# Softmax sums of a full attention: two running sums with every third tile added by an accumulating DMA, and three groups of totals on TensorE, in place of eight short sums and nine groups

## The reference

```python
qkv = (x @ qkv_w + qkv_b).reshape(Bw, Nw, 3, nh, dh)      # Nw = 3136 tokens, nh = 8 heads, dh = 32
q, k, v = (qkv[:, :, 0], qkv[:, :, 1], qkv[:, :, 2])
attn = jnp.einsum('bnhd,bmhd->bhnm', q * scale, k)
bias = jnp.transpose(rpb_table[rel_idx], (2, 0, 1))
attn = jax.nn.softmax(attn + bias[None], axis=-1)
out = jnp.einsum('bhnm,bmhd->bnhd', attn, v).reshape(Bw, Nw, Cd)
```

## Time and profile before

| | |
|---|---|
| median of 3 runs | 6850.28 us (6849.53 to 6852.86) |
| profiled execution, its own time | 6852.2 us |
| its span, first to last instruction | 6850.3 us |
| mean granted TensorE clock | 0.95 |
| PE busy | 5952.2 us (87%) |
| PE weight loads | 3529.1 us (52%) |
| DVE busy | 4462.8 us (65%) |
| ACT busy | 3207.0 us (47%) |
| POOL busy | 4402.5 us (64%) |

### The profile page before, as it was taken

How to read it: one execution, slowest core, us unless ns; L and a number is a source line. 1 busy time by engine, 2 the same in 40 slices (tenths; PEclk the granted TensorE clock), 3 DMA queues, 4 the chain that set the end, 5 groups by cost and what they waited for, 6 DMA issues and landing times. The chain is left out here.

```text
span 6850.3 us, 123297 instructions
## 1 busy us (share of the span) xinstructions
PE 5952.2 (87%) x37974; PEld 3529.1 (52%) x37974; DVE 4462.8 (65%) x8532; ACT 3207.0 (47%) x6574; POOL 4402.5 (64%) x1492
## 2 busy tenths in 40 slices
PE   2777767769999999999999999999999999442878
PEld 2666545545555555555555555555555554231555
DVE  2666633357777777777777777777777775684000
ACT  1444411106666665666666666666666666000111
POOL 0222222228888888888888888888888888443332
PEclk9999989969999999999999999999999999675988
DMA  1111144441101101111100100110110000332221
GB/s 38 45 42 44 39 140 163 155 124 44 32 15 33 46 15 33 30 32 33 30 24 24 46 24 23 33 39 23 33 32 20 17 15 8 104 112 65 46 47 24
DMA packets 217803, 323.95 MB, mean 47 GB/s; under 512 B 43392, under 2 KB 182628, under 8 KB 214244
## 3 DMA queue, kind: packets, MB, share of 16 engines
q1 hardware_dynamic: 201084, 295.76, 15.1%
q0 software_dynamic: 13568, 19.39, 1.5%
q10 hardware_dynamic: 2664, 2.62, 0.2%
HBM read 179.93 MB, written 137.35 MB: 46 GB/s over the span
## 5 line engine op out<-in xcount | busy, mean ns | idle before, releaser
L1193 DVE TENSOR_REDUCE tops<-ps_m 128x1 f32<-128x448 f32 (+1 forms) x5600 | 3120.5, 618 | 911.3 <-PE ps_m L1096 860.2
L1169 ACT ACTIVATE prob<-ps_s 128x448 f32<-128x448 f32 (+1 forms) x5600 | 2619.8, 550 | 1748.0 <-PE ps_s L1032 1708.7
L1002 POOL TENSOR_TENSOR tile_sum<-prob 128x1792 f32<-128x1792 f32 x448 | 1802.4, 4023 | 664.3 <-ACT prob L1169 664.0
L1032 PE MATMUL ps_s<-queries,keys 97*128 97x448 f32 (+1 forms) x5600 | 2200.2, 397 | 15.4 <-ACT prob L1169 7.6
L1096 PE MATMUL ps_m<-keys,queries 96*128 96x448 f32 (+1 forms) x5600 | 2092.2, 381 | 35.4 <-DMA keys<-k_parts 20.2
L1002 POOL TENSOR_TENSOR tile_sum<-tile_sum,prob 128x1792 f32<-128x1792 f32 x448 | 1807.8, 4035 | 31.8
L1032 PEld LDWEIGHTS ps_s<-queries,keys 97*128 97x128 f32 (+1 forms) x5600 | 1042.2, 187 | 1158.0 <-ACT prob L1169 660.7
L1048 PE MATMUL ps_o<-prob,values 128*32 128x448 f32 x11200 | 1343.1, 551 | 2.9 <-ACT prob L1169 1.2
L1096 PEld LDWEIGHTS ps_m<-keys,queries 96*128 96x128 f32 (+1 forms) x5600 | 1062.6, 190 | 240.2 <-DVE tops L1193 84.8
L257 POOL TENSOR_TENSOR logit<-logit,top 112x896 f32<-112x896 f32 x112 | 188.4, 1683 | 557.3 <-DVE top L374 557.3
L1060 PE MATMUL ps_d<-tile_sum,ones 128*32 128x448 f32 x3584 | 421.6, 542 | 3.2 <-POOL tile_sum L1002 3.2
(11 more groups left out here) (171 smaller groups left out, 4670.4 us busy)
## 6 DMA issues: line engine op xcount, KB each, us to landing
queries<-q_parts SPq DMA_DIRECT2D x288, 160.0 KB, 3.2
keys<-k_parts SPq DMA_DIRECT2D x96, 392.0 KB, 6.9
xT<-in_x SPq DMA_DIRECT2D x56, 224.0 KB, 2.5
window_out<-oT SPq DMA_DIRECT2D x56, 224.0 KB, 2.0
aT<-window_out SPq DMA_DIRECT2D x56, 224.0 KB, 3.7
hidden<-h SPq DMA_DIRECT2D x28, 448.0 KB, 4.4
q_parts<-hi SPq DMA_DIRECT2D x56, 224.0 KB, 1.9
q_parts<-lo SPq DMA_DIRECT2D x56, 224.0 KB, 2.0
```

The source lines that it names most:

```text
L1002: nc.gpsimd.tensor_tensor(tile_sum[k % 2][:, :, :], left, prob[:, t % SLOTS, :, :], ALU.add).then_inc(summed, 1)
L1032: mm = nc.tensor.matmul(o[:, 0:CH], keys[x.u][:, j, at:at + k], queries[x.v][:, j, own:own + CH], start=True, stop=not last, skip_group_ch ...
L1169: nc.scalar.activation(prob[0:k, t % SLOTS, j, :], ps_s[0:k, score_bank(x.hm, i), 0:CH], ACT.Exp).then_inc(exp_done, 1)
L1193: nc.vector.tensor_reduce(tops[0:rows, j, r - blocks[0], c:c + 1], ps_m[0:rows, e % MB, 0:CH], AX.X, ALU.max).then_inc(m_used, 1)
```

## The change

- The short tile of 64 keys moves from first to last (`keys_of`, `load_values`, the memset of `values`), the corner of the bias goes with the last full tile, and the memset of `prob` goes.
- The 24 full tiles make eight triples. Triple k belongs to running sum k % 2, and each of the two sums goes on through four triples of a half instead of starting anew. Of a triple GpSimd adds the first two tiles (in triples 0 and 1 one add makes the sum, in the others there are two), and the third is added by a DMA from `prob` to `tile_sum` with `accum_op=ALU.add`, issued by GpSimd itself after it has waited for the add and for the third tile's exponentials. 14 adds and 8 such DMAs a half.
- A new pair of semaphores, `moved_in[0]` and `moved_in[1]`, counts those DMAs. The next add to the same sum waits for it, so do the totals, and so does the exponential that takes over a third tile's slot.
- Three groups of totals a half: sum 0, the short tile, sum 1, after scores 99, 111 and 111 (11 of the next half). The waits of GpSimd on totals are left at triples 0 and 1 alone.
- `normalize` comes after tile 22's add instead of tile 21's.

```diff
-SUM_TILES = [(1, 2, 3, 4)] + [(t, t + 1, t + 2) for t in range(5, 23, 3)] + [(23, 24)]
+TRIPLES = [(t, t + 1, t + 2) for t in range(0, KT - 1, 3)]
...
+        moved_in = [ctx.enter_context(nc.semaphore(f"moved_in{a}")) for a in range(2)]
-        D_ITEMS = SUMS + 1
+        D_ITEMS = 3
-        NORMALIZE_AT = 21
+        NORMALIZE_AT = 22
...
-            return (0, FIRST) if t == 0 else (FIRST + 128 * (t - 1), 128)
+            return (0, FIRST) if t == KT - 1 else (FIRST + 128 * t, 128)
...
-                for k, tiles in enumerate(SUM_TILES):
-                    if x.has_before or k > 1:
-                        pool.wait_ge(d_used, ONE + x.h * D_ITEMS + (k if k > 1 else k - 1))
-                    for before, t in zip(tiles, tiles[1:]):
-                        pool.wait_ge(exp_done, ONE + x.h * TILES + HG * (t + 1))
-                        left = prob[:, before % SLOTS, :, :]
-                        if before != tiles[0]:
-                            pool.wait_ge(summed, ONE + x.h * ADDS_HALF + n)
-                            left = tile_sum[k % 2][:, :, :]
-                        nc.gpsimd.tensor_tensor(tile_sum[k % 2][:, :, :], left, prob[:, t % SLOTS, :, :],
+                for k, (first, second, third) in enumerate(TRIPLES):
+                    total = tile_sum[k % 2][:, :, :]
+                    if k < 2:
+                        if x.has_before:
+                            pool.wait_ge(d_used, ONE + x.h * D_ITEMS - 2 * (1 - k))
+                        pool.wait_ge(exp_done, ONE + x.h * TILES + HG * (second + 1))
+                        nc.gpsimd.tensor_tensor(total, prob[:, first % SLOTS, :, :], prob[:, second % SLOTS, :, :],
                                                 ALU.add).then_inc(summed, 1)
                         n += 1
-                        if t == NORMALIZE_AT and x.has_before:
-                            normalize(x.h - 1, 1 - x.v)
+                    else:
+                        pool.wait_ge(moved_in[k % 2], 16 * (x.h * MOVES_HALF + k // 2))
+                        for t in (first, second):
+                            pool.wait_ge(exp_done, ONE + x.h * TILES + HG * (t + 1))
+                            if t == second:
+                                pool.wait_ge(summed, ONE + x.h * ADDS_HALF + n)
+                            nc.gpsimd.tensor_tensor(total, total, prob[:, t % SLOTS, :, :], ALU.add).then_inc(summed, 1)
+                            n += 1
+                            if t == NORMALIZE_AT and x.has_before:
+                                normalize(x.h - 1, 1 - x.v)
+                    pool.wait_ge(summed, ONE + x.h * ADDS_HALF + n)
+                    pool.wait_ge(exp_done, ONE + x.h * TILES + HG * (third + 1))
+                    nc.gpsimd.nop(nofuse=True)
+                    nc.gpsimd.dma_start(total, prob[:, third % SLOTS, :, :], accum_op=ALU.add).then_inc(moved_in[k % 2], 16)
...
-                else:
-                    pe.wait_ge(summed, ONE + x.h * ADDS_HALF + sum(ADDS[:k]))
+                if k != 1:
+                    pe.wait_ge(moved_in[k // 2], 16 * MOVES_HALF * (x.h + 1))
...
-            for k, tiles in enumerate(SUM_TILES):
-                i = HG * tiles[-1] + 15
+            for k, last in ((0, TRIPLES[-2][-1]), (1, TRIPLES[-1][-1]), (2, TRIPLES[-1][-1])):
+                i = HG * (last + 1) + 12
...
+                        if user == KT - 1:
+                            act.wait_ge(d_used, ONE + h * D_ITEMS + 2)
+                        elif place == 2:
+                            act.wait_ge(moved_in[triple % 2], 16 * (h * MOVES_HALF + triple // 2 + 1))
+                        else:
+                            act.wait_ge(summed, ONE + h * ADDS_HALF + added(user))
```

More of the change, by code:

```diff
@@ L811, in full_attention @@
         assert ENTRIES % MB == 0
-        ADDS = [len(tiles) - 1 for tiles in SUM_TILES]
-        ADDS_HALF = sum(ADDS)
+        ADDS_HALF = 2 * len(TRIPLES) - 2
+        MOVES_HALF = len(TRIPLES) // 2
         start_counts(nc, sems, {tile_used: BEHIND})
@@ L873, in added @@
         def added(t):
[L876 to L880, removed]
+            k, place = divmod(t, 3)
+            return k + 1 if k < 2 else 2 * k - 1 + place
         @block.sync
@@ L1029, in score @@
                 o = ps_s[0:k, score_bank(x.hm, i), :]
-                last = t == KT - 1 and x.s == 0
+                last = t == KT - 2 and x.s == 0
                 own = (CH * x.s) % BLK
@@ L1055, in total @@
                     pe.wait_ge(den_kept, ONE + x.h)
-                else:
-                    pe.wait_ge(summed, ONE + x.h * ADDS_HALF + sum(ADDS[:k]))
+                if k != 1:
+                    pe.wait_ge(moved_in[k // 2], 16 * MOVES_HALF * (x.h + 1))
                 for j in range(HG):
-                    moving = prob[:, 0, j, :] if k == 0 else tile_sum[(k - 1) % 2][:, j, :]
-                    mm = nc.tensor.matmul(ps_d[j * DH:(j + 1) * DH, 0:CH], ones[:, int(k > 0), :], moving,
-                                          start=(k == 0), stop=(k == SUMS))
+                    moving = prob[:, (KT - 1) % SLOTS, j, :] if k == 1 else tile_sum[k // 2][:, j, :]
+                    mm = nc.tensor.matmul(ps_d[j * DH:(j + 1) * DH, 0:CH], ones[:, int(k != 1), :], moving,
+                                          start=(k == 0), stop=(k == D_ITEMS - 1))
                 mm.then_inc(d_used, 1)
@@ L1106, in _ @@
                 bursts[i % TILES].append((weigh, t, i >= TILES))
[L1107 to L1109 removed]
+            for k, last in ((0, TRIPLES[-2][-1]), (1, TRIPLES[-1][-1]), (2, TRIPLES[-1][-1])):
+                i = HG * (last + 1) + 12
                 while not bursts[i % TILES]:
                     i += 1
[L1112 removed]
+                bursts[i % TILES].append((total, k, i >= TILES))
             for i in bursts:
@@ L1159, in half @@
                     act.wait_ge(tile_used, ONE + x.h * KT + t)
-                    if t > SLOTS:
-                        act.wait_ge(summed, ONE + x.h * ADDS_HALF + added(t - SLOTS))
-                    elif t == SLOTS:
-                        act.wait_ge(d_used, ONE + x.h * D_ITEMS + 1)
-                    elif x.has_before:
-                        act.wait_ge(summed, ONE + (x.h - 1) * ADDS_HALF + added(t + KT - SLOTS))
+                    if t >= SLOTS or x.has_before:
+                        h, user = (x.h, t - SLOTS) if t >= SLOTS else (x.h - 1, t + KT - SLOTS)
+                        triple, place = divmod(user, 3)
+                        if user == KT - 1:
[4 more added lines that the diff above has]
+                            act.wait_ge(summed, ONE + h * ADDS_HALF + added(user))
                     for j in range(HG):
@@ L1235, in _ @@
             for u in range(2):
-                nc.vector.memset(values[u][FIRST:128, 0, :], 0.0).then_inc(ones_set, 1)
-            nc.vector.memset(prob[FIRST:128, 0, :, :], 0.0).then_inc(ones_set, 1)
+                nc.vector.memset(values[u][FIRST:128, KT - 1, :], 0.0).then_inc(ones_set, 1)
             dve.wait_ge(tops_set, ONE + 2)
```

7 lines of the change are left out of this document (3 added, 4 removed).

## The result

The changed kernel takes **7525.6 us** (median of 4 runs, 7523.5 to 7527.2), the kernel before 6851.15: ratio 1.098, 95% interval 1.0965 to 1.1003. It is slower, as forecast, but by 674 us where 90 were forecast, far above the range of 6690 to 7160.

The account below looks back on a forecast made before the run. TensorE bounds the kernel at 76.8 us a half; the change saves it 4.6, but a ring through GpSimd's adds and DMAs takes 78.25. 56 x 1.45 = +81 us, plus some 9 once, gives 6940 us, range 6690 to 7160.

Parts of the forecast that it names:

- TensorE's bound: Attention stretch: TensorE's own instructions set 76.8 us a half; without six groups of totals 72.2, at most -255 us.
- the price of a total: TensorE's matmuls for one group of totals: 0.76 us each, nine groups a half becoming three.
- c: GpSimd's time for issuing one accumulating DMA: taken as 1.4 us, six of them in the sum for a half.
- L: Time from the end of an accumulating DMA's issue until its bytes have landed: taken as 6.5 us.
- The lag of GpSimd from triple 2 to 7: GpSimd needs 9.6 us a triple where three tiles give 8.2 to 8.7, so it falls behind until the last total.
- the ring's line "the normalize in triple 7: 1.15": Term of the per-half sum: normalize counted as 1.15 us of GpSimd's time in triple 7.
- The sign that was named: In the profile after, TensorE's total on the second sum waits for tile_sum's DMA, some 3 us in each half.
- TensorE is about to wait for the same DMA anyway: At the start of a half, reason for costing SP's query loads at nothing; without that cover up to L in 3 of 7 halves.
- The ring through the last total: GpSimd's triples 2 to 7, last DMA's landing, last total, next half's tile 6: 63.35 + 6c + L = 78.25 us a half.
- 1 (faster): Rival: ring shorter than TensorE's time because a direct DMA may hold GpSimd less; 6694 us, chance 0.30.
- 3 (no change): Rival: gain and ring cancel, within 0.2% of the time before; 6850 us, chance 0.06.
- 2 (slow transfers, 7248): Rival: DMAs move at the accumulating packets' own rate, L = 9.4 and c = 1.83; 7248 us, chance 0.14.

Follow-up runs that it names:

- e12: Changed kernel with rows before SP's store, earlier normalize and reciprocals, tiles 10, 20, 23 straight into the totals, 13 adds, six DMAs a half: 6731.1 us, 0.982 of before.
- e1: Changed kernel with both pairs of shift rows issued ahead of the store in SP's list: 7220.6 us, 1.054 of the kernel before.
- e2: Changed kernel with normalize after tile 21's add instead of tile 22's: 7156.1 us, 1.044 of the kernel before.
- e8: Changed kernel with normalize after tile 19's add instead of tile 22's, and VectorE's reciprocal pieces from score 28 on: 7162.6 us, 1.044 of the kernel before.
- e4: Kernel before, without accumulating DMAs, with normalize after tile 24's add instead of tile 21's: 7330.2 us, 1.070 of the kernel before.

## Why the prediction was wrong

- **TensorE's bound and the price of a total: right.** 0.76 us each; e12 with three groups fewer gives 74.4 us a half.
- **c: right in size.** GpSimd's triples follow every 9.67 us, so c = 9.67 - 8.20 = 1.47 (taken: 1.4). In the trace that is 0.62 us from the end of the add to the issue, 0.61 us from the issue's start to the next add, and two adds that take 8.44 us instead of 8.20.
- **L: right in the middle of a half, too low where the sum uses it.** The median landing is 6.4 us from the issue's start, 5.8 after the 0.6 us that GpSimd is held by it (taken: 6.5). The page "DMA: Bandwidth & Descriptors" of the Trainium skill (section Anatomy of one DMA) gives by estimate 4.1 us for this size; the trace says 6.4, and the measurement decides. Its 1 us to the first byte, for the emission (section Latency and other measured facts), is nearer to the 0.87 us of an issue than to the 1.47 us that GpSimd loses. But the sum asks for triple 7's DMA, which flies beside SP's loads. From issue to landing that one took 8.0 us in the mean of the change's 56 halves, 9.0 in e1, 10.1 in e2 and 9.8 in e8.
- **The lag of GpSimd from triple 2 to 7: right**, and so is that the gain of 255 us turns into waits.
- **The step that failed is the ring's line "the normalize in triple 7: 1.15": what GpSimd's lag does to SP was never followed.** The normalize entered the sum as GpSimd's time and nothing else. It also releases SP's store, and behind the store stand the second pair of rows and the query loads. The text named SP's loads only as traffic beside the last DMA: "I cost that at nothing". Measured: 363 us (change against e8), and 482 us when the coupling alone is put into the kernel before (e4).
- **The cost of a wait on TensorE was taken as its length.** With the clock at half behind it, TensorE was busy 4.9 us a half longer in the change and 4.2 us in e8 than its matmuls take at full clock. The sum had no term for this.
- **The sign that was named did not come.** The total of the second sum was to wait some 3 us in each half. In the change it waited in one half of 56, since the late rows stopped TensorE first.
- **"TensorE is about to wait for the same DMA anyway" failed.** In e1 the late query loads cost 156.9 us of waits, nothing hid them, and the loads stretch the DMA that TensorE waits for (7.8, 9.4 and 13.1 us at the turns shown instead of 6.4).
- The ring through the last total was one of two; the first sum's total after score 99 closed as tight a one.

By size, of the 674 us: 363 go with the coupling over SP, and 311 are e8's loss. Of those 311 the clock at 4.2 us a half is some 235 and leaves some 75, near the 81 of the forecast. That nearness is in part chance: e8's halves wait at either total, and longer landings than forecast stand against shorter terms elsewhere. The 363 also hold clock, and e8's normalize stands ahead of triple 6's DMA, which may cost it something, so the cut between the two parts is rough.

The rivals: 1 (faster) and 3 (no change) are out. 2 (slow transfers, 7248) had a time nearer the result. Its reason, the accumulating packets' own rate, isn't there, since a DMA that flies alone lands after 6.4 us; landings as long as its L did come, from the loads beside. That the kernel became slower was forecast by a ring that did not bind in it; e2 and e8, in which TensorE hardly waits for the rows, stay at 7156 and 7163 with waits at both totals, so this ring and its twin make it slower by themselves.

## What to carry to other kernels

When an engine is going to be late, list everything that its late instructions release on *other* queues, and what stands behind the released one there: a store that waits for its semaphore in an engine's fixed list holds back every load behind it in that list. Put such a store last, or its release early; one add's place was worth 370 us here (e2). And a DMA that stands between an engine and its next work belongs in the middle of a stage, not at its turn, where the loads of the next stage are in flight as well.

## What was not expected of the hardware

- TensorE's granted clock stood at half while it waited and behind the wait: 0.52 in 3226 to 3232 us of the change, behind a wait of 7.3 us, and 0.50 in 3190 to 3195 of e8, behind one of 2.6 us. The mean clock of the attention went from 1.00 to 0.90 in the change.
- GpSimd gives up 1.47 us for a direct accumulating DMA of 128 rows of 7 KB, though the issue's own row says 0.87. The next add starts 0.61 us after the issue does, but 0.62 us pass between the add before and the issue, and the adds are 0.24 us longer for two. For 512 rows of 64 bytes the issue is 1.29 us.
- An accumulating DMA from SBUF to SBUF of 896 KB landed 6.3 us after its issue at the least; of 224 KB 3.1, of 32 KB 2.9. Beside loads of queries and keys one of 896 KB took 13.1 us.
- 2 KB rows with which TensorE went on 2.4 us after their issue in a quiet moment (e4) needed 7.3 us beside one such DMA.
